# Preparing an attention layer inside the product before it, block by block, with its stores and reloads on GpSimd's queue

## The chip, the cores and the metric

The kernel runs on one core of a Trainium2 chip. The time is device microseconds (us) of one execution on that core. A core has TensorE (PE, matrix products), VectorE (DVE), ScalarE (ACT), GpSimd (POOL) and SyncE (SP), which run their own instruction streams and meet at semaphores, and 16 DMA engines that all queues share. SP and ACT issue DMAs through hardware queues, POOL through a software queue.

## What is computed

Four graph layers over 3125 nodes with 64 features and 100000 edges, each with a layer norm and a ReLU ahead and added to its input:

```
h = relu(layernorm(x));  x = x + smoothing(h)      # three propagations over the edges
h = relu(layernorm(x));  x = x + sage(h)           # one weighted propagation
h = relu(layernorm(x));  x = x + gated_cheb(h)     # two propagations, then (1 - sigmoid(.)) * tanh(.)
h = relu(layernorm(x))
q, k, v = h[src] @ qTrans, h[dst] @ kTrans, h[dst] @ vTrans      # 4 heads of 16
att = exp(clip(sum(q * k, per head), -10, 10))
x = x + segment_sum(att / (segment_sum(att, src)[src] + 1e-8) * v, src)
```

## The kernel before, in words

The nodes are padded to 3200, 25 tiles of 128. The program has three blocks (`nc.Block`), and each ends at a barrier of all five engines: no engine starts the next block before every engine has come to the end of its own stream in this one.

1. `build_matrices` sorts the edges into two dense 3200 x 3200 float matrices in DRAM, `weights_dram` and `counts_dram`. Its scatters are GpSimd's indirect DMAs (L620).
2. `propagating_layers` does six products with these matrices (`prop` 0 to 5; the last, 5, is `CHEB2`). A product goes by seven blocks of columns, `CHUNKS`: six of 512 and one of 128. Four wide blocks (0, 2, 3, 5) are streamed by SP into `ring`, blocks 1 and 4 (`KEPT`) stay in `resident`, block 6 in `last`. On PE a block `n` is 25 matmuls (L969); after the fifth or sixth of them (`s == after`; later in block 6) `by_nodes` (L942) turns the sums of block `n - 1` back to nodes by rows. DVE then finishes the nodes of block `n - 1` (L896 to L905), with ACT's Sigmoid and Tanh between (L773, L775).
3. `attention_layer` has a prologue and a main part. The prologue does for all 25 tiles at once: layer norm (L666 to L674), transposes (L1248), the product with qTrans and kTrans (L1252) and with vTrans (L1257), copies, and the split of q and k into three bf16 parts (L1152, L1155: cast, subtract, cast, subtract, cast). SP stores each part into `parts_dram` (L1073) and loads it again as six groups of 16 rows for q and six for k (L1081), so that one bf16 matmul with 96 rows gives a float-like product. PE waits for all twelve loads (L1262). The main part then goes over chunks of 512 query nodes and, in each, over 25 tiles: scores (L1275), transposed counts (L1282), ACT's exponentials, DVE's clips and products (L1168 to L1176), and values (L1290).

## Time and profile before

| | us |
|---|---|
| median of 3 runs (lowest and highest) | 2656.49 (2653.78 to 2657.03) |
| the profiled execution's own time | 2654.28 |
| its span, first to last instruction | 2652.6 |
| PE busy | 1194.4 (45%) |
| DVE busy | 1843.7 (70%) |
| ACT busy | 776.8 (29%) |
| POOL busy | 1266.3 (48%) |

The shares are means over three stages of a different nature. The first block takes a little over half the span; the change lies at the seam of the second and third. So the stage must be read by itself, in windows of the trace, by its chain of waits: which instruction released which, in order of time. PEq, DVEq and SPq are an engine's sequencer (branches, semaphores, DMA issues).

### The profile page before, as it was taken

What the parts mean: (1) busy time and instruction counts of PE and PEld (TensorE: products, weight loads), DVE (VectorE), ACT (ScalarE), POOL (GpSimd) and SP (SyncE); (2) the same over time, 40 slices, a digit from 0 to 9 for tenths busy, and PEclk for the clock granted to TensorE, in tenths of its full rate; (3) what the DMA queues carried; (4) which work ended last, traced back from release to release, by engine and by line L of the source; (5) the groups of instructions that cost most, each with busy time, mean ns of one, the idle gap of its engine ahead of it and who ended that gap; (6) DMA issues with size and microseconds to landing.
All of it is one profiled execution on the core that took longest, in us unless ns stands there. A gap on an engine that the chain in (4) does not pass through costs nothing. (4 is left out here: it accounts for less than half of the span.)

```text
span 2652.6 us, 40013 instructions
## 1 busy us (share of the span) xinstructions
PE 1194.4 (45%) x12261; PEld 593.1 (22%) x12261; DVE 1843.7 (70%) x3893; ACT 776.8 (29%) x1905; POOL 1266.3 (48%) x973
## 2 busy tenths in 40 slices
PE   1111111111111111111111049999999559989997
PEld 1111111111111111111111013344444313333334
DVE  9988888888888888888888210023211549999997
ACT  0000000132233222311112220000001159999996
POOL 2688888888888888888888600000000000000001
PEclk6555555555555555555555569999999769999997
DMA  7777777588898888767566699889978363333331
GB/s 229 238 202 224 206 210 221 112 212 216 211 226 196 223 211 215 180 139 178 107 165 155 124 372 423 363 362 388 423 286 349 55 120 87 87 87 87 87 87 46
DMA packets 487296, 537.82 MB, mean 203 GB/s; under 512 B 130048, under 2 KB 443709, under 8 KB 469053
## 3 DMA queue, kind: packets, MB, share of 16 engines
q1 hardware_dynamic: 124717, 290.41, 30.2%
q10 hardware_dynamic: 249904, 245.78, 28.7%
q0 software_dynamic: 112608, 0.85, 10.1%
q8 instruction: 28, 0.46, 0.1%
q14 instruction: 39, 0.32, 0.0%
HBM read 368.64 MB, written 168.31 MB: 202 GB/s over the span
## 5 line engine op out<-in xcount | busy, mean ns | idle before, releaser
L620 POOL DMA_INDIRECT table<-amount,cell x782 | 1210.6, 1548 | 294.4 <-issue 278.3
L441 DVE SCALAR_TENSOR_TENSOR equal<-key_row,keys,masks 128x1280 bf16<-128x1280 f32 (+9 forms) x790 | 692.0, 941 | 0.2 <-DVE parts L427 0.2
L573 PE MATMUL totals<-parts_g,equal 128*128 128x6 bf16 x4345 | 128.6, 168 | 1022.8 <-DVE is_tile L450 1022.8
L291 ACT ACTIVATE w_tile<-cells 128x128 f32<-128x128 f32 x600 | 179.2, 301 | 779.5 <-issue 768.8
L573 PEld LDWEIGHTS totals<-parts_g,equal 128*128 128x128 bf16 x4345 | 122.0, 104 | 1034.2 <-DVE is_tile L450 1034.2
L969 PE MATMUL banks<-ring,xs 128*64 128x512 f32 x1200 | 290.9, 601 | 92.7 <-DMA ring<-counts_dram 91.3
L1237 POOL COPY v_tile<-v_all 128x128 f32 x175 | 51.2, 294 | 506.6 <-PE banks_d L1290 433.8
L1227 POOL MEMSET o_t<- 128x64 f32 x1 | 0.2, 151 | 565.2 <-POOLq L731 565.2
L433 DVE SCALAR_TENSOR_TENSOR equal_tail<-key_row,keys,masks 128x1280 bf16<-128x1280 f32 x156 | 235.2, 1545 | 20.6 <-issue 17.5
L1275 PE MATMUL banks_d<-q,k 96*128 (+2 forms) x700 | 194.7, 371 | 75.5 <-DMA k<-parts_dram 46.5
L1122 ACT ACTIVATE att<-banks_d,shift 128x1024 f32<-128x1024 f32 (+1 forms) x175 | 198.7, 1135 | 76.6 <-PE banks_d L1275 76.0
L1127 ACT ACTIVATE att<-att,shift 128x1024 f32<-128x1024 f32 (+1 forms) x175 | 206.6, 1181 | 0.0
L1173 DVE SCALAR_TENSOR_TENSOR att<-att,banks_d 128x1024 f32<-128x1024 f32 (+1 forms) x175 | 190.1, 1086 | 11.4 <-ACT att L1127 4.4
L1176 DVE TENSOR_TENSOR att<-att,banks_d 128x1024 f32<-128x1024 f32 (+1 forms) x175 | 189.0, 1080 | 0.0
L1125 ACT ACTIVATE att<-banks_d 128x1024 f32<-128x1024 f32 (+1 forms) x175 | 183.4, 1048 | 0.0
L1290 PE MATMUL banks_d<-att,v_tile 128*32 128x512 f32 (+1 forms) x1400 | 173.3, 571 | 0.5 <-DVE att L1176 0.5
L458 DVE TENSOR_REDUCE amount<-totals 128x20 f32<-128x60 f32 x79 | 17.3, 219 | 203.9 <-POOLq L634 203.9
L969 PEld LDWEIGHTS banks<-ring,xs 128*64 128x64 f32 x1200 | 93.4, 138 | 263.8 <-issue 149.4
L1168 DVE TENSOR_SCALAR att<-att 128x1024 f32<-128x1024 f32 (+1 forms) x175 | 108.9, 622 | 55.8 <-ACT att L1125 55.1
L969 PE MATMUL banks<-resident,xs 128*64 128x512 f32 x600 | 145.1, 596 | 2.9 <-DMA resident<-counts_dram 2.5
L291 ACT ACT_TABLE_LOAD x1 | 1.3, 1283 | 489.5 <-POOLq L634 489.5
L582 PE MATMUL totals<-carried_parts,equal_tail 128*128 128x6 bf16 x1560 | 54.2, 168 | 199.5 <-DVE carried_parts L478 199.5
(225 smaller groups left out, 1501.0 us busy)
## 6 DMA issues: line engine op xcount, KB each, us to landing
table<-zeros ACTq DMA_DIRECT2D x100, 800.0 KB
cells<-table ACTq DMA_DIRECT2D x24, 3200.0 KB, 12.1
ring<-counts_dram SPq DMA_DIRECT2D x60, 1280.0 KB, 11.7
ring<-weights_dram SPq DMA_DIRECT2D x60, 1280.0 KB, 10.5
key_row<-keys_dram SPq DMA_DIRECT2D x79, 640.0 KB
weights_dram<-w_tile ACTq DMA_DIRECT2D x24, 1600.0 KB
counts_dram<-c_tile ACTq DMA_DIRECT2D x24, 1600.0 KB
count<-counts_dram SPq DMA_DIRECT2D x150, 256.0 KB, 2.9
```

Of the source, the lines that this page charges most:

```text
L291: ins = nc.scalar.activation(w_tile[:, b, s], cells[:, s, :, 0], ACT.Copy, accum_out=deg_parts[:, s, bass.ds(t, 1)])
L433: ins = nc.vector.scalar_tensor_tensor(equal_tail[:, b, i, :], key_row[:, b, :], keys[:, bass.ds(g * G - TAIL + i, 1)], all_mask, ALU.is_e ...
L441: ins = nc.vector.scalar_tensor_tensor(equal[b][:, OWN_AT[j]:OWN_AT[j + 1]], key_row[:, b, j * P:GE], keys[:, bass.ds(g * G + j, 1)], own_ ...
L573: nc.tensor.matmul(sums, equal[b][:, at:at + P], parts_g[:, b, j, :], start=False, stop=True, skip_group_check=True)
L620: nc.gpsimd.indirect_dma_start(out=table, out_offset=bass.IndirectOffsetOnAxis(ap=cell[:, b, j:j + 1], axis=0), in_=amount[:, b, j, :], in ...
L969: ins = nc.tensor.matmul(banks[at:at + D, g % 2, 0:w], xs[:, prop % 2, s], rows, start=s < 2, stop=True, skip_group_check=True)
L1122: nc.scalar.activation(att[:, j, high, 0:W], scores[:, high, 0:W], ACT.Relu, bias=shift[:, 0:1]).then_inc(scores_read[1], 1)
L1125: nc.scalar.activation(att[:, j, low, 0:W], scores[:, low, 0:W], ACT.Exp).then_inc(scores_read[0], 1)
L1127: nc.scalar.activation(att[:, j, high, 0:W], att[:, j, high, 0:W], ACT.Exp, bias=shift[:, 1:2]).then_inc(expd_high, 1)
L1173: nc.vector.scalar_tensor_tensor(att[:, j, high, 0:W], att[:, j, high, 0:W], HI, times, ALU.min, ALU.mult)
L1176: nc.vector.tensor_tensor(att[:, j, low, 0:W], att[:, j, low, 0:W], times, ALU.mult).then_inc(weighted, 1)
L1275: ins = nc.tensor.matmul(scores[:, hd, 0:W], k6[:, hd, bass.ds(t * P, P)], q6[:, hd, bass.ds(ci * BANK, W)], start=True, stop=True)
```

## The change

The attention's prologue moves into the last product of the block before. For a block `n` of nodes:

- DVE, right after it has finished the nodes of block `n`, normalises them (`normalise`, as the earlier layers do), with ACT's Sqrt between, and then splits block `n - 1` (`split`).
- PE, in block `n` (from 2 on), transposes block `n - 2` of `h` after `by_nodes` (`turn_next`), and eight matmuls later projects it (`project`). The last two blocks are done behind the product.
- ACT copies the transposed block (`copy_h`) and the values (`copy_values`, into `k["acc"]`).
- GpSimd, for each block: waits for the three parts, stores them with one DMA, waits until that has landed, and issues twelve loads of 16 rows, each 4 heads x 512 columns (6 x 2 row groups; seven blocks, so 7 stores and 84 loads in place of 3 and 12). It starts when the product's block 1 is done, for the rows lie where `resident` had that block.
- In the attention block, PE waits for `rows_placed[0]` alone, and waits for the later blocks of rows at tiles 4, 8, 12, 16, 20 and 24 of its first chunk, which is written out without a loop (`first=True`). GpSimd copies the values per tile from `acc` into `v_tile`, in strides.
- Some buffers share space for that: `zeros` lies in `k["acc"]`, and `cells`, `w_tile`, the first resident block and the rows all in `k["held"]`.

```diff
+            def copy_h(n):
+                w = CHUNKS[n][1]
+                act.wait_ge(h_turned, n + 1)
+                if n:
+                    act.wait_ge(values_made, n)
+                nc.scalar.copy(h_t[0:D, 0:w], TURN[:, 0:w]).then_inc(h_copied, 1)
...
                         if before[0] == CHEB2:
-                            gates_of(before[1])
+                            if n >= 2:
+                                copy_h(n - 2)
+                            gates_of(n - 1)
+                            root(2, n - 1)
+                            if n >= 2:
+                                copy_values(n - 2)
...
+            def split(n):
+
+                w = CHUNKS[n][1]
+                dve.wait_ge(projected, n + 1)
+                if n >= 2:
+                    dve.wait_ge(rows_stored[n - 2], 16)
+                left = PROJECTED[n % 2][:, 0:w]
+                for i in range(3):
+                    part = parts[:, n % 2, i, 0:w]
+                    if i == 2:
+                        nc.vector.tensor_copy(part, left).then_inc(parts_ready, 1)
+                        break
+                    nc.vector.tensor_copy(part, left).then_inc(parts_step, 1)
+                    dve.wait_ge(parts_step, 4 * n + 2 * i + 1)
+                    nc.vector.tensor_tensor(rest[:, 0:w], left, part, ALU.subtract).then_inc(parts_step, 1)
+                    dve.wait_ge(parts_step, 4 * n + 2 * i + 2)
+                    left = rest[:, 0:w]
+                dve.wait_ge(parts_ready, n + 1)
...
                         link(nc.vector.tensor_tensor(x[:, ts], x[:, ts], narrow, ALU.add))
+                        normalise(ts, tiles, 2 * NC + n)
+                        dve.sem_inc(h_ready, 1)
+                        if n:
+                            split(n - 1)
+            split(NC - 1)
...
+            def project(n):
...
+                nc.tensor.matmul(PROJECTED[n % 2][:, 0:w], k["qk"][:], h_t[0:D, 0:w], start=True, stop=True
+                                 ).then_inc(projected, 1)
+                for j in range(tiles):
+                    ins = nc.tensor.matmul(VALUES[n % 2][:, j * D:(j + 1) * D], h_t[0:D, j * P:(j + 1) * P], k["v"][:],
+                                           start=True, stop=True, skip_group_check=True)
+                ins.then_inc(values_made, 1)
...
+                            if prop == CHEB2 and n >= 2:
+                                turn_next(n - 2)
+                        if prop == CHEB2 and n >= 2 and s == later:
+                            project(n - 2)
             by_nodes(CHEB2, NC - 1)
...
+            for n in (NC - 2, NC - 1):
+                turn_next(n)
+                project(n)
+
+        @block.gpsimd
+        def _(pool):
+            pool.wait_ge(sums_ready, NC * CHEB2 + KEPT[0] + 1)
+            for n, (c0, w) in enumerate(CHUNKS):
+                cols = slice(c0, c0 + w)
+                pool.wait_ge(parts_ready, n + 1)
+                pool.dma_start(parts_dram[:, :, :, :, cols].rearrange("i w h d n -> (w h d) i n"), parts[:, n % 2, :, 0:w]
+                               ).then_inc(rows_stored[n], 16)
+                pool.wait_ge(rows_stored[n], 16)
+                for side, part_of in ((1, KPART), (0, QPART)):
+                    for i in range(NPART):
+                        pool.dma_start(placed[side][i * HD:(i + 1) * HD, :, cols],
+                                       parts_dram[part_of[i], side, :, :, cols].rearrange("h d n -> d h n")
+                                       ).then_inc(rows_placed[n], 16)
...
-            layer_norm(nc, dve, link, x, h, tmp, stat, var_ready, std_ready, 0)
-            dve.sem_inc(h_ready, 1)
...
-            pe.wait_ge(v_copied, 1)
             pe.wait_ge(consts_set, 2)
-            pe.wait_ge(rows_placed, 16 * 2 * NPART)
+            pe.wait_ge(rows_placed[0], 16 * 2 * NPART)
...
+                    if first:
+                        for t in range(2, T):
+                            if t * P % BANK == 0:
+                                pe.wait_ge(rows_placed[t * P // BANK], 16 * 2 * NPART)
+                            step(t, t % RING, t // RING)
+                        return
```

PE in the last product, its fifth block (`resident`), before:

```order
L969 MATMUL banks<-resident,xs 64x512 [waits sums_read]
L969 MATMUL banks<-resident,xs 64x512 x4
L942 MATMUL banks<-cheb,y_t 128x128 [waits sums_read,post_read]
L942 MATMUL banks<-cheb,y_t 128x128 x3
L969 MATMUL banks<-resident,xs 64x512 x20
```

and now, the same place (L1063 is the product, L1009 `by_nodes`, L1022 `turn_next`, L1032 and L1035 `project`):

```order
L1063 MATMUL banks<-resident,xs 64x512 [waits sums_read]
L1063 MATMUL banks<-resident,xs 64x512 x4
L1009 MATMUL banks<-cheb,y_t 128x128 [waits sums_read,post_read]
L1009 MATMUL banks<-cheb,y_t 128x128 x3
L1022 MATMUL banks<-ident,h 64x128 [waits h_ready_c,h_copied_c]
L1022 MATMUL banks<-ident,h 64x128 x3
L1063 MATMUL banks<-resident,xs 64x512 x8
L1032 MATMUL banks<-h_t,qk 128x512 [waits values_copied,parts_step,h_copied_c]
L1035 MATMUL banks<-v,h_t 128x64 x4
L1063 MATMUL banks<-resident,xs 64x512 x12
```

Nine more instructions stand in the block: four transposes, one wide product and four narrow ones.

ACT in the last product, one block of it, before (L773 and L775 are Sigmoid and Tanh):

```order
L773 ACTIVATE term<-acc 128x4x64 [waits gate_ready]
L775 ACTIVATE term<-h 128x4x64
```

and now, a block from 2 on:

```order
L802 COPY h_t<-banks 64x512 [waits values_made,h_turned_c]
L793 ACT_TABLE_LOAD
L793 ACTIVATE term<-acc 128x4x64 [waits gate_ready]
L795 ACTIVATE term<-h 128x4x64
L788 ACT_TABLE_LOAD
L788 ACTIVATE stat<-stat 128x4 [waits var_ready]
L807 COPY acc<-banks 128x256 [waits values_made]
```

The function tables are loaded twice in each block, once ahead of Sigmoid and once ahead of Sqrt.

GpSimd between the barrier after `build_matrices` and the attention's first copies, before:

```order
L1224 UNCONDITIONAL_BRANCH [waits barrier_Pool_Activation_PE_DVE_SP_gather]
L1227 MEMSET o_t 128x64
L1228 MEMSET v_all 128x3200
L1230 MEMSET v_all 128x100 [waits v_cleared]
```

and now (the first two of seven blocks, and the seventh with what follows it):

```order
L1093 DMA parts_dram<-xs 128x3x512 [waits parts_ready,sums_ready]
L1098 DMA held<-parts_dram 16x4x512 [waits rows_stored0]
L1098 DMA held<-parts_dram 16x4x512 x11
L1093 DMA parts_dram<-xs 128x3x512 [waits parts_ready]
L1098 DMA held<-parts_dram 16x4x512 [waits rows_stored1]
L1098 DMA held<-parts_dram 16x4x512 x11
```

```order
L1093 DMA parts_dram<-xs 128x3x128 [waits parts_ready]
L1098 DMA held<-parts_dram 16x4x128 [waits rows_stored6]
L1098 DMA held<-parts_dram 16x4x128 x11
L751 UNCONDITIONAL_BRANCH
L1280 UNCONDITIONAL_BRANCH [waits barrier_Pool_Activation_PE_DVE_SP_gather]
L1284 MEMSET v_tile 128x640
```

All 91 DMAs stand ahead of the barrier in GpSimd's stream, each store behind the twelve loads of the block before it.

## Rows read from the trace of the kernel before

**Rows 1.** Chain that ended last, 1950 to 2165 us: start us, us, what.
```profile
2074.74 1.83 DVE stat L666
...
2084.93 4.34 PE banks_d L1248 x25
...
2108.08 22.40 DMA parts_dram<-qk_part
...
2130.84 19.23 DMA k<-parts_dram
...
2150.22 0.06 PEldq L1263
...
2150.44 2.97 DMA count<-counts_dram
```

**Rows 2.** Waits, 2060 to 2156 us: waited for, us in total, times, longest.
```profile
PE banks_d L1275 <- DMA k<-parts_dram: 46.5, 1, 46.5
...
DVE stat L666 <- PEq L731: 0.5, 1, 0.5
```

**Rows 3.** Timeline of PE, 1960 to 2075 us: start us, us, instruction.
```profile
1966.62 0.60 PE L916 MATMUL banks<-ident,h 128*64 128x128 f32 x4
...
2020.37 1.16 PE L942 MATMUL banks<-cheb,y_t 128*128 128x128 f32 x8
...
2056.98 1.16 PE L942 MATMUL banks<-cheb,y_t 128*128 128x128 f32 x8
...
2069.20 1.53 PE L969 MATMUL banks<-last_chunk,xs 128*64 128x128 f32 x24
```

**Rows 4.** Timeline of all engines, 2040 to 2165 us.
```profile
2044.58 1.16 PE L942 MATMUL banks<-cheb,y_t 128*128 128x128 f32 x8
...
2045.85 0.69 DVE L896 TENSOR_TENSOR term<-banks,scale 128x512 f32<-128x512 f32 x1 [8.66 <-PE banks L942]
...
2048.58 0.42 DVE L905 TENSOR_TENSOR x_nodes<-x_nodes,term 128x256 f32<-128x256 f32 x1
...
2074.71 1.28 ACT L1109 ACT_TABLE_LOAD   x1 [1.02 <-PEq L731]
...
2086.03 0.58 ACT L1046 COPY h_t_d<-banks_d 64x512 f32<-64x512 f32 x1 [3.42 <-PE banks_d L1248]
```

**Rows 5.** Groups by line, 2071 to 2156 us: busy us, mean ns, idle before.
```profile
L1257 PE MATMUL banks_d<-v,h_t_d 64*128 64x64 f32 x50 | 8.5, 350 | 0.7 <-DVE qk_t L1049 0.7
...
L1155 DVE TENSOR_TENSOR qk_t<-qk_t,qk_part 128x3200 f32<-128x3200 f32 x2 | 7.0, 3493 | 0.1
...
L1252 PE MATMUL banks_d<-h_t_d,qk 64*128 64x512 f32 (+1 forms) x14 | 5.6, 551 | 0.0
L1152 DVE CAST qk_part<-qk_t 128x3200 bf16<-128x3200 f32 x3 | 5.5, 1827 | 0.2
...
L1049 DVE COPY qk_t<-banks_d 128x512 f32<-128x512 f32 x3 | 2.1, 691 | 3.4 <-PE banks_d L1252 3.4
```

**Rows 6.** Line 840 alone: ns min/median/max, first and last start us.
```profile
L840 DVE TENSOR_REDUCE stat<-x_nodes x14: 219/420/421, 1753.6 to 1909.7; 128x4 f32<-128x256 f32 x12, 128x1 f32<-128x64 f32 x2
```

**Rows 7.** Line 620, GpSimd's DMAs, alone.
```profile
L620 POOL DMA_INDIRECT table<-amount,cell x782: 1546/1546/2582, 47.7 to 1508.0; - x196
```

**Rows 8.** Timeline of POOL, 1000 to 1040 us.
```profile
1007.12 1.55 POOL L620 DMA_INDIRECT table<-amount,cell  x1 [0.30 <-issue]
1008.97 1.55 POOL L620 DMA_INDIRECT table<-amount,cell  x1 [0.30 <-issue]
```

**Rows 9.** Line 1081 alone, SP's loads of the rows.
```profile
L1081 SPq DMA_DIRECT2D k<-parts_dram x6: 303/427/467, 2105.1 to 2130.8; - x6
```

**Rows 10.** Line 1073 alone, SP's stores of the parts.
```profile
DMA to landing us min/median/max: 3.3/4.7/22.4
```

**Rows 11.** DMA, 2108 to 2130.8 us.
```profile
DMA packets 631, 3.30 MB, mean 145 GB/s; under 512 B 115, under 2 KB 115, under 8 KB 630
```

More of the change, by code:

```diff
@@ L72, in by_chunk, with rows_of @@
     return dram[c0 * NR:(c0 + w) * NR].rearrange("(p s c) -> p s c", p=P, s=T)
+def rows_of(k):
+    half = T * BANK // 2
+    return [k["held"][0:NPART * HD, w * half:(w + 1) * half].bitcast(BF16).rearrange("p (h n) -> p h n", h=HEADS)
+            for w in range(2)]
 def gnn_layers(nc, x, src, dst, edge_weight, W_self, b_self, W_neigh, b_neigh,
@@ L90, in gnn_layers @@
             "stat": sb("stat", [P, 3, T], F32),
+            "acc": sb("acc", [P, T, D], F32),
+            "held": sb("held", [P, T * BANK], F32),
             "ident": sb("ident", [P, P], F32),
@@ L101, in gnn_layers @@
         }
+        parts_dram = nc.dram_tensor("parts_dram", [3, 2, HEADS, HD, NR], BF16, kind="Internal").ap()
+        rows_placed = [ctx.enter_context(nc.semaphore(f"rows_placed{n}")) for n in range(len(CHUNKS))]
         with ExitStack() as c:
@@ L154, in build_matrices @@
     amount = sb("amount", [P, 2, G, 2], F32, c)
-    cells = sb("cells", [P, T, P, 2], F32, c)
-    w_tile, c_tile = sb("w_tile", [P, 2, T, P], F32, c), sb("c_tile", [P, 2, T, P], F32, c)
+    cells = k["held"][:, 0:2 * NR].rearrange("p (s c two) -> p s c two", c=P, two=2)
+    w_tile = k["held"][:, 2 * NR:4 * NR].rearrange("p (b s c) -> p b s c", b=2, c=P)
+    c_tile = sb("c_tile", [P, 2, T, P], F32, c)
     deg_parts = sb("deg_parts", [P, T, T], F32, c)
@@ L684, in propagating_layers @@
     xs = sb("xs", [P, 2, T, D], F32, c)
-    acc = sb("acc", [P, T, D], F32, c)
+    acc = k["acc"]
     gates = (acc, h)
@@ L692, in propagating_layers @@
     ring = sb("ring", [P, PIECES, PIECE, BANK], F32, c)
-    resident = sb("resident", [P, len(KEPT), T, BANK], F32, c)
+    resident = [k["held"][:].rearrange("p (s c) -> p s c", c=BANK), sb("resident", [P, T, BANK], F32, c)[:]]
+    rest = term[:].rearrange("p t f -> p (t f)")
+    parts = xs[:, 0].rearrange("p t f -> p (t f)")[:, 0:3 * BANK].bitcast(BF16).rearrange("p (b n c) -> p b n c", b=2, n=3)
+    placed = rows_of(k)
     last = sb("last_chunk", [P, T, P], F32, c)
@@ L714, in propagating_layers @@
     last_landed = sem("last_landed")
+    h_ready, h_turned, h_copied = sem("h_ready_c"), sem("h_turned_c"), sem("h_copied_c")
+    projected, values_made, values_copied = sem("projected"), sem("values_made"), sem("values_copied")
+    parts_step, parts_ready = sem("parts_step"), sem("parts_ready")
+    rows_stored = [sem(f"rows_stored{n}") for n in range(len(CHUNKS))]
     def tiles_of(n):
@@ L944, in by_nodes, with turn_next @@
                 ins.then_inc(post_filled, 1)
+            def turn_next(n):
+                ts = tiles_of(n)
+                if n:
+                    pe.wait_ge(h_copied, n)
+                else:
+                    pe.wait_ge(turned_copied, 2 * NC)
+                pe.wait_ge(h_ready, n + 1)
+                for j, t in enumerate(range(ts.start, ts.stop)):
+                    ins = nc.tensor.transpose(TURN[:, j * P:(j + 1) * P], h[:, t], k["ident"][:])
+                ins.then_inc(h_turned, 1)
+            def project(n):
+                w, tiles = CHUNKS[n][1], CHUNKS[n][1] // P
+                pe.wait_ge(h_copied, n + 1)
+                if n >= 2:
+                    pe.wait_ge(parts_step, 4 * (n - 2) + 2)
+                    pe.wait_ge(values_copied, n - 1)
+                nc.tensor.matmul(PROJECTED[n % 2][:, 0:w], k["qk"][:], h_t[0:D, 0:w], start=True, stop=True
[4 more added lines that the diff above has]
+                ins.then_inc(values_made, 1)
             for prop in range(6):
@@ L951, in _ @@
                     after = (T // 2 if n == NC - 1 else PIECE) // 2 * 2 + 1 - g % 2
+                    later = after + 8
                     for s in range(T):
@@ L960, in _ @@
                                 pe.wait_ge(kept_landed[KEPT.index(n)][q], 16 * (prop // 3) + 16)
-                            rows = resident[:, KEPT.index(n), s]
+                            rows = resident[KEPT.index(n)][:, s]
                         else:
@@ L1107, in _ @@
         def _(act):
-            act.wait_ge(var_ready, 1)
-            nc.scalar.activation(stat[:, 2], stat[:, 1], ACT.Sqrt).then_inc(std_ready, 1)
-            copy_banks(act, nc.scalar.copy, 0)
             act.wait_ge(consts_set, 2)
@@ L1315, in steps, with chunk @@
                 return scores_of, tiles, values_of
-            def chunk(ci, width, next_width):
-                scores_of, tiles, values_of = steps(ci, width)
+            def chunk(ci, width, next_width, first=False):
+                scores_of, tiles, values_of = steps(ci, width, first)
                 tiles()
@@ L1329, in _ @@
                 steps(0, 4)[0](t)
-            with pe.Fori(0, SC - 1) as ci:
+            chunk(0, 4, 4, first=True)
+            with pe.Fori(1, SC - 1) as ci:
                 chunk(ci, 4, 4)
```

119 lines of the change are left out of this document (34 added, 85 removed).

## The prediction, on record before the changed kernel ran

> **What bounds the kernel now.** I read the page's slices first. DVE and GpSimd fill the first stage, PE the second and DVE the third, and between the second and the third lie slices with every engine low: the attention's prologue. What it costs is read from the chain of waits [rows 1]. The barrier holds DVE for 0.5 us [rows 2], from 2074.2 on; then one engine at a time works: layer norm (from 2074.7), transposes and projections (from 2084.9), the split (to 2108.1) [rows 1]. From there to 2150.1 nothing computes: the third store lands 22.40 us after its issue and the last load of rows 19.23 us after its own. PE passes its gate at 2150.2 [rows 1], after 46.5 us of waiting [rows 2]. So 76 us lie between the two stages, 42 of them DMA. The gate is the one point that counts: behind it the attention is DVE's, tile by tile, and its instructions are not touched, so that a gate passed x us earlier is worth x us. In the last product PE is the bound; its blocks follow at (2056.98 - 2020.37) / 3 = 12.2 us [rows 3].
>
> **What the change adds to the product (paid).** Per wide block PE gets four transposes, 0.60 [rows 3]; the wide product, 5.6 / 6.25 = 0.9; four narrow pairs, 8.5 / 25 x 4 = 1.4 [rows 5]. The sum is 2.9 us. Blocks 2 to 6 of the product each carry one set, so it ends 5 x 2.9 = 14.5 us later, at 2070.7 + 14.5 = 2085.2 [rows 3], with blocks 15.1 us apart. All of it is PE's; that the product is not slowed further I take from DVE having 8.66 us idle in a block [rows 4], and the bound of this is nothing to 14.5 us if a DMA wait of PE hides some.
>
> **When the parts of a block are ready.** `by_nodes` of a block starts at 2044.58 and DVE adds the result to x until 2049.0 [rows 4], 4.4 us later. ACT now loads a table between (1.28 [rows 4]); it comes after ACT's copy of h (0.58 [rows 4]) and so holds Sigmoid up by about 1.1. The normalisation is five operations of 0.42 [rows 6], with small ones and links between, 2.9 us; the Sqrt table loads beside it. The split by block: cast and subtract from PSUM at 0.69 each (the nearest is L1049, 691 ns), then from SBUF 1827 x 512 / 3200 = 0.29, 3493 x 512 / 3200 = 0.56 and 0.29 [rows 5], 2.6 with the links. Block 0 is projected in PE's third block, at about 2026, earlier than DVE gets there. So its parts are ready at 2020.4 + 4.4 + 1.1 + 2.9 + 2.6 = 2031.4, the next ones 15 us apart (2046, 2061, 2076), block 4's at about 2090, and blocks 5 and 6, behind the product with two further table loads and a chain through four engines, at about 2096 and 2097.
>
> **GpSimd's queue.** It decides. Per block it issues a store, waits until that has landed, and issues twelve loads; 91 DMAs all stand ahead of the barrier, which no engine passes without GpSimd. So the waits for single blocks in the attention's first chunk never bind: when PE gets there, all loads have been issued. The trace has no plain DMA from this queue. The nearest rows:
> - one load (64 rows of 1 KB). Below: SP's issue of 64 rows, 0.43 [rows 9]. Above: GpSimd's indirect DMA of 128 rows, 1.55 [rows 7] with 0.30 between, a period of 1.85 [rows 8]. That one reads its addresses as well. I take half of it for half the rows, 0.93.
> - the store (384 rows): issue 1.85, as one indirect DMA (0.34 as SP's, 5.6 for three times the rows). Landing: 3.3, the least of L1073 [rows 10], which moved twice the bytes.
>
> A block costs S = 1.9 + 3.3 + 12 x 0.93 = 16.3 us, more than the 15 at which blocks come. The queue is never empty after the first: it ends at 2031.4 + 7 x 16.3 = 2145.5. With the barrier (0.5) and DVE's constants, now behind it (0.4), PE's gate is passed at 2146.4 instead of 2150.2: -3.8 us. The first count tile and the exponentials' table load follow the gate as before. GpSimd's one small copy per tile stays one small copy. The first chunk without a loop and the shared buffers I cost at nothing: the one stands beside DVE's work, the others move no instruction; if PE fetched its longer code late, it would be a few us.
>
> So the change removes 76 us of serial work, pays 14.5 to the product and about 12 behind it, and the queue gives most of the rest back. Profiled: span 2652.6 - 3.8 = 2648.8, own time 2650.5. The runs' median stands 2.2 above the profiled time: 2656.5 - 3.8 = 2652.7, so **2653 us**. About 0.2% (5.3 us) is what a measurement here can tell from no change.
>
> Every us in S is 7 us in the end. It breaks even at S = (2150.2 - 0.9 - 2031.4) / 7 = 16.8, a load of 0.97 us. The bounds: with SP's issue times S = 0.34 + 3.3 + 5.2 = 8.8, and the queue waits for the parts until block 4 (2090 + 3 x 8.8 = 2116.4, the gate at 2117.3): -33 us, 2624. With the dearest of all, S = 5.6 + 3.3 + 22.2 = 31.1: 2031.4 + 217.7 = 2249: +100 us.
>
> **A rule that speaks against it.** L1152, a cast from SBUF, took 1827 ns for 3200 elements, L1155 3493 [rows 5]: the cast runs at nearly twice the rate. By the Trainium skill ("SBUF — State Buffer", "SBUF: two separate sides"), GpSimd cannot write descriptors while VectorE runs an operation in its two-port mode. No row here shows plain DMAs of GpSimd beside such a cast. If that held in full, two casts of 0.29 would add 0.6 to each S, 4 us in all, and turn the -3.8 into 0. The same skill ("DMA: Bandwidth & Descriptors", "Latency and other measured facts") gives about 1 us to the first byte of a DMA from this queue; taken as a load's issue time, as an estimate, it would give S = 17.2 and +3 us.
>
> **Rivals.**
> - Cheap issue. The 1.55 us are mostly for the addresses of an indirect DMA; a plain one of 64 rows costs 0.65 (between 0.43 and 0.93), the store 0.5. S = 11.6, and blocks wait for their parts: block 4 ends at 2101.6, block 6 at 2124.8, the gate at 2125.7, -24.5 us, **2632**. For it: SP needs only 0.43 for the same rows [rows 9]. Against it: the software queue's only row is four times that [rows 7].
> - Dear issue, the other side. The cost is nearly one per DMA, not per row: 1.25, midway between 0.65 and the 1.85 of rows 8. S = 1.9 + 3.3 + 15 = 20.2, the queue ends at 2172.8, the gate at 2173.7, +23.5 us, **2680**. GpSimd would then work for 140 us while the other engines stand at the barrier for 75. It decides from 0.97 us on. For it: 782 indirect DMAs never took less than 1546 ns [rows 7]. Against it: these have twice the rows and more to read.
> - Store behind loads, slower too. In the old prologue the DMA engines were full at 145 GB/s [rows 11], 9 GB/s each, and the third store took 22.4 us behind the loads of 6400 B rows [rows 1]. By bytes, a block's loads (786 KB) take 5.4 us at that rate, less than their issue, and the next store waits for the last one alone. If a row of 1 KB cost half of the 6400 / 9.06 = 706 ns of a long one, 48 rows per engine would take 17 us, the next store would land behind them, and S = 17 + 1.9 + 3.3 = 22: +39 us, **2695**. It decides from 0.24 us per row. Against it: a DMA's cost by bytes fits the other transfers.
>
> **Chances.** My forecast (S from 15.3 to 17.7) 0.34, cheap issue 0.28, dear issue 0.30, store behind loads 0.08. Of the forecast's 0.34, 0.13 is faster by over 0.2% (S under 16.05), 0.20 within it, 0.01 slower. So faster 0.41, same 0.20, slower 0.39. The range goes from the lower bound's side, 2624, to the third rival, 2695; that leaves out the dearest issues and little else. The forecast's own range is 2646 to 2659.
>
> **What would show it.** PE's blocks 2 to 5 of the last product 15 us apart and its end near 2085 (right), or 12 to 13 apart (a DMA wait hid it). First store of parts from GpSimd near 2031. The period of GpSimd's loads: 0.93 as forecast, under 0.8 the first rival, over 1.1 the second. From a store's issue to the first load 3 to 5 us; 10 or more is the third. All engines but GpSimd idle from about 2098 to the barrier. No wait of PE for rows in the first chunk. A gate of PE at 2146 with the attention of the same length; the forecast is wrong if the attention itself changes by more than 3 us, or if the first two blocks of the program, untouched in their instructions, move.

## The result and the profile after

The changed kernel takes 2637.40 us (median of 4 runs, 2635.66 to 2641.44), the kernel before 2655.39 beside it (median of 4, 2653.78 to 2657.03). The ratio is 0.993, with a 95% interval of 0.9917 to 0.9943: 18 us or 0.7% faster. The prediction said 2653 and faster with a chance of 0.41; the result lies in its range (2624 to 2695), but outside the forecast's own (2646 to 2659). The profiled execution took 2636.98 us, its span is 2635.3.

The first score of attention is the gate. PE's timeline around it, after (start us, us, instruction):

```profile
2102.49 0.52 PE L1035 MATMUL banks<-v,h_t 64*128 64x64 f32 x2
2135.27 1.01 PE L1317 MATMUL banks_d<-held 96*128 96x512 bf16 x2 [32.25 <-ACTq L1184]
```

Before, the first score stood at 2150.47, right behind the gate of [rows 1]. So 15.2 of the 17.3 us of span come from an earlier gate, and 2.1 from attention itself (500.0 instead of 502.1 us; on these 2.1 see the experiment with the looped chunk). Who is waited for now? The waits from 2030 to 2140 us, after (waited for: us in total, times, longest), to be read beside [rows 2]:

```profile
POOL held L1098 <- DMA parts_dram<-xs: 37.5, 7, 17.2
...
PE banks_d L1317 <- ACTq L1184: 32.3, 1, 32.3
...
DVE zero_row_d L1213 <- PEq L751: 28.9, 1, 28.9
...
POOL v_tile L1284 <- POOLq L751: 7.7, 1, 7.7
```

PE, ACT and DVE all stand at the barrier for about 30 us, and no engine waits for the rows of a block in attention. The engine that holds the barrier is GpSimd. Its whole timeline from the first parts on:

```profile
2040.56 0.86 POOL L1093 DMA_DIRECT2D parts_dram<-xs  x1 [521.69 <-DVE xs L905]
2050.08 6.36 POOL L1098 DMA_DIRECT2D held<-parts_dram  x12 [8.67 <-DMA parts_dram<-xs]
2056.43 0.78 POOL L1093 DMA_DIRECT2D parts_dram<-xs  x1
2074.40 6.09 POOL L1098 DMA_DIRECT2D held<-parts_dram  x12 [17.20 <-DMA parts_dram<-xs]
2080.48 0.77 POOL L1093 DMA_DIRECT2D parts_dram<-xs  x1
2083.73 6.09 POOL L1098 DMA_DIRECT2D held<-parts_dram  x12 [2.48 <-DMA parts_dram<-xs]
2089.82 0.77 POOL L1093 DMA_DIRECT2D parts_dram<-xs  x1
...
2118.21 0.77 POOL L1093 DMA_DIRECT2D parts_dram<-xs  x1
2120.72 6.09 POOL L1098 DMA_DIRECT2D held<-parts_dram  x12 [1.74 <-DMA parts_dram<-xs]
2134.56 0.63 POOL L1284 MEMSET v_tile<- 128x640 f32 x1 [7.75 <-POOLq L751]
```

The loads alone (duration min/median/max in ns, first and last start):

```profile
L1098 POOL DMA_DIRECT2D held<-parts_dram x84: 514/514/692, 2050.1 to 2126.3; - x84
```

The reader is to see four things. After its first store GpSimd never waits for parts; how near it comes to waiting is told in the part on the prediction. A block's cycle in the quiet part is 2089.82 - 2080.48 = 9.3 us, not 16.3: a load's issue is 6.09 / 12 = 0.51 us and a store's 0.77. The first two stores are waited for during 8.67 and 17.20 us instead of 2.48. And there are 7.75 us between the end of the last load's issue and the barrier. What the core's DMA engines did meanwhile stands in the windows of after (start:end, length, then busy time of PE, PEld, DVE, ACT and POOL, TensorE's granted clock, DMA share, GB/s):

```profile
2041.00:2050.00 9.00, 9.00 (x47) 3.87 (x43) 3.54 (x8) 4.45 (x6) 0.41 (x1) 1.00 1.00 391
2056.00:2074.00 18.00, 18.00 (x96) 7.93 (x94) 8.03 (x18) 5.41 (x9) 1.21 (x2) 1.00 0.97 286
2100.00:2127.00 27.00, 1.51 (x5) 1.06 (x5) 4.88 (x14) 0.94 (x4) 20.11 (x39) 0.50 0.38 100
2128.50:2134.50 6.00, 0.00 (x0) 0.00 (x0) 0.00 (x0) 0.00 (x0) 0.00 (x0) 0.50 0.00 0
```

The two slow stores went while the DMA engines were full (share 1.00 and 0.97), mostly with SyncE's stream of matrix tiles; beside the second one block 0's own loads were under way too, which needed up to 15.0 us to land. And in the last 6 us ahead of the barrier nothing is done by any engine or any DMA.

Line 632 alone is the scatter of the first stage, GpSimd's indirect DMA (duration min/median/max in ns, first and last start), the counterpart of [rows 7]:

```profile
L632 POOL DMA_INDIRECT table<-amount,cell x782: 1550/1559/2572, 48.3 to 1517.3; - x196
```

This stage's instructions are the same, and yet its median is 13 ns longer, and its last scatter starts at 1517.3 instead of 1508.0. PE's first product behind it starts 9.2 us later (1569.03 against 1559.84), and in the last product `by_nodes` of block 1 still comes 8.3 later (2028.63 against the 2020.37 of [rows 3]). PE's last product itself went by rows such as these:

```profile
2029.62 0.60 PE L1022 MATMUL banks<-ident,h 128*64 128x128 f32 x4
...
2033.73 1.12 PE L1032 MATMUL banks<-h_t,qk 64*128 64x512 f32 x2
2034.70 1.00 PE L1035 MATMUL banks<-v,h_t 64*128 64x64 f32 x8
...
2073.39 0.60 PE L1022 MATMUL banks<-ident,h 128*64 128x128 f32 x4
```

Three blocks take 2073.39 - 2029.62 = 43.8 us, 14.6 each, against 12.2 in [rows 3].

### The profile page after: what moved, and what is told of

Read it like the earlier page. It is cut to its first block and busy times, and to the rows that moved or that the text cites. A ratio compares the mean times of both kernels' runs of the same rounds, so it can differ in the third digit from the quotient of the medians.

```text
span 2635.3 us, 40047 instructions
## 1 busy us (share of the span) xinstructions
PE 1193.1 (45%) x12261; PEld 590.7 (22%) x12261; DVE 1857.5 (70%) x3958; ACT 795.0 (30%) x1929; POOL 1312.5 (50%) x1064
## 5 line engine op out<-in xcount | busy, mean ns | idle before, releaser
L303 ACT ACTIVATE held<-held 128x128 f32<-128x128 f32 x600 | 179.2, 301 | 787.2 <-issue 776.4
L1063 PE MATMUL banks<-ring,xs 128*64 128x512 f32 x1200 | 290.5, 600 | 93.0 <-DMA ring<-counts_dram 91.7
L1093 POOL DMA_DIRECT2D parts_dram<-xs x7 | 5.5, 783 | 521.7 <-DVE xs L905 521.7
L1294 POOL COPY v_tile<-acc 128x64 f32 x175 | 41.5, 238 | 441.1 <-PE banks_d L1332 440.5
L1317 PE MATMUL banks_d<-held 96*128 (+2 forms) x700 | 192.9, 366 | 65.7 <-ACT att L1195 32.4
L1063 PEld LDWEIGHTS banks<-ring,xs 128*64 128x64 f32 x1200 | 92.9, 137 | 261.9 <-issue 147.7
L836 ACT COPY y_t<-banks 128x512 f32<-128x512 f32 (+1 forms) x42 | 22.7, 540 | 340.6 <-PE banks L1063 340.6
L925 DVE TENSOR_TENSOR xs<-banks,scale 128x256 f32<-128x256 f32 (+1 forms) x14 | 5.5, 396 | 164.1 <-PE banks L1009 164.1
```

The costliest lines, as they stand in the source:

```text
L303: ins = nc.scalar.activation(w_tile[:, b, s], cells[:, s, :, 0], ACT.Copy, accum_out=deg_parts[:, s, bass.ds(t, 1)])
L1063: ins = nc.tensor.matmul(banks[at:at + D, g % 2, 0:w], xs[:, prop % 2, s], rows, start=s < 2, stop=True, skip_group_check=True)
L1317: ins = nc.tensor.matmul(scores[:, hd, 0:W], k6[:, hd, bass.ds(t * P, P)], q6[:, hd, bass.ds(ci * BANK, W)], start=True, stop=True)
```

## The experiments

Eleven kernels ran. The question was where the queue's 28 saved us went, and whether GpSimd is the engine to issue these DMAs. Beside each time stands its ratio to the kernel before of the same chip, with the 95% interval.

**SyncE issues instead of GpSimd.** The changed kernel; the loop of stores and loads stands at the end of SyncE's part of the same block, behind its last tile of the matrix:

```
-        @block.gpsimd
-        def _(pool):
-            pool.wait_ge(sums_ready, NC * CHEB2 + KEPT[0] + 1)
+            sp.wait_ge(sums_ready, NC * CHEB2 + KEPT[0] + 1)
...
-                pool.dma_start(parts_dram[...]
+                sp.dma_start(parts_dram[...]
```

> The changed kernel with its 7 stores and 84 loads issued by SP, behind SP's last stream, instead of by GpSimd; all else as changed. In the changed kernel GpSimd issued a load each 0.51 us and a block of rows took 9.35 us (0.77 store, 2.48 landing, 6.1 loads); its last load was issued at 2126.8 and the barrier opened 7.7 us later. Theory A (GpSimd's own end of stream costs some 7 us, and the queue the rest): SP issues a load in 0.43 us, the last parts are ready at about 2105.7 in the changed trace's time, the last block follows one block behind it (3.3 + 5.2), and the barrier opens 0.5 us after the last issue: PE's gate about 13 us earlier than in the changed kernel. If the first stage also returns to its old length, 9 us more: 2615 to 2625 us. Rival B (the barrier waits for the rows' landing or for something that any queue has): the gate moves by 0 to 5 us, 2632 to 2637 us. Rival C (hardware queue fills the DMA engines with 16-partition loads at 145 GB/s, stores land late behind them): not faster or slower than the changed kernel.

Measured: 2617.02 us (4 runs), 0.9864 [0.9849, 0.9879]: 20.4 us below the changed kernel's median, or 18.6 when each is taken against the kernel before on its own chip. Its scatters, SyncE's timeline and GpSimd's next instruction:

```profile
L632 POOL DMA_INDIRECT table<-amount,cell x782: 1546/1547/2512, 47.6 to 1508.3; - x196
```

```profile
2048.22 0.53 SPq L783 DMA_DIRECT2D parts_dram<-xs  x1
2058.26 5.67 SPq L788 DMA_DIRECT2D held<-parts_dram  x12
...
2106.34 0.43 SPq L783 DMA_DIRECT2D parts_dram<-xs  x1
2108.26 5.46 SPq L788 DMA_DIRECT2D held<-parts_dram  x12
2114.82 32.66 SPq L1165 DMA_DIRECT2D count<-counts_dram  x16
```

```profile
2114.12 0.63 POOL L1281 MEMSET v_tile<- 128x640 f32 x1 [604.30 <-POOLq L751]
```

The first score stands at 2114.84, 20.4 us earlier than in the changed kernel (attention then takes 501.0 instead of 500.0). These 20.4 us come apart in three. The first stage is 9.0 shorter (last scatter 1508.3 against 1517.3). SyncE's last issue ends at 2113.72, which is 2126.81 - 9.0 - 2113.72 = 4.1 earlier than GpSimd's would without that shift, though SyncE, busy with the matrix until 2048.1, issues its first store 16.7 us later by that measure: a load costs it 0.46 (5.46 / 12), a block in the quiet part 8.1 to 9.1. And GpSimd's first clear of attention, at 2114.12, follows this end by 0.4 instead of 7.75. Together 9.0 + 4.1 + 7.35 = 20.4. So the projection inside the product is worth 36.6 us, and about half of that hangs on who issues its DMAs. Theory A had the size, and rivals B and C fall.

**The shared buffers alone.** The kernel before, with only the buffers of the change (`held` and `acc` in place of `zeros`, `cells`, `w_tile`, the old `acc`, the first resident block, `q6` and `k6`); nothing is moved in time:

```
-    q6, k6 = sb("q6", [NPART * HD, HEADS, NR], BF16, c), sb("k6", ...)
+    q6, k6 = rows_of(k)
...
-    cells = sb("cells", [P, T, P, 2], F32, c)
+    cells = k["held"][:, 0:2 * NR].rearrange(...)
```

> The kernel before with only the shared buffers of the change (zeros in acc; cells, w_tile, the first resident block and the rows in held). Question: the first stage became 9 us longer in the changed kernel (GpSimd's indirect DMAs 1559 ns instead of 1546, 782 of them). Theory A, the place of the buffers does it: indirect DMAs at about 1559 ns, total +8 to +10 us over before. Rival B, it comes with GpSimd's plain DMAs or differs from run to run: indirect DMAs at 1546 ns, total as before within 3 us.

Measured: 2653.89 us (11 runs), 1.0002 [0.9993, 1.0011], scatters at 1546 ns with the last at 1509.2. The addresses cost nothing; the 9 us are not theirs. (The profiled execution was the slowest of the eleven, 2662.06 us, and its scatters are as short as those of the kernel before; it is met again under the looped chunk.)

**The old prologue's DMAs from GpSimd.** The kernel before, with its 15 stores and loads of the rows (the only ones of [rows 9, 10]) issued by GpSimd:

```
-            def keep(part_no):                         # in SyncE's attention
-                sp.dma_start(parts_dram[part_no]...
+            def keep(part_no):                         # in GpSimd's attention
+                pool.dma_start(parts_dram[part_no]...
```

> The kernel before with its old prologue, where GpSimd instead of SP issues the 3 stores and 12 loads of whole rows (6400 B). Theory A (the cost of GpSimd's plain DMA is about 0.5 to 0.8 us each and rows land at the same pace as from SP): the prologue is bound by landing, so within 3 us of before if the first stage stays. If plain DMAs in GpSimd's stream are what lengthens the first stage's indirect DMAs (1559 instead of 1546 ns): +9 us on top. Rival B (each plain DMA costs 1.3 to 1.9 us): the twelve loads cost 15 to 23 us of issue, of which the DMA landing hides most, total +3 to +8 us without any change in the first stage.

Measured: 2662.20 us (5 runs), 1.0035 [1.0022, 1.0049]: 8.6 us slower. Line 620 of it:

```profile
L620 POOL DMA_INDIRECT table<-amount,cell x782: 1549/1558/2557, 48.3 to 1518.1; - x196
```

Its plain DMAs run 600 us after the last scatter, in another block of the program, and still each scatter is 12 ns longer and the last starts 10 us later. This separates the effect from anything else in the change. A second place in this trace bears on the rule on the two-port mode. The timeline of all engines:

```profile
2113.88 1.55 POOL L1222 DMA_DIRECT2D q<-parts_dram  x3
2115.42 3.09 POOL L1222 DMA_DIRECT2D k<-parts_dram  x3
2116.58 1.83 DVE L1132 CAST qk_part<-qk_t 128x3200 bf16<-128x3200 f32 x1
```

Three loads take 1.55 us where no cast runs, and 3.09 beside one: GpSimd was held up by about 1.5 us, nearly the cast's 1.83. By the Trainium skill ("SBUF — State Buffer", "SBUF: two separate sides") GpSimd can't write descriptors while VectorE works in its two-port mode; this row agrees. In the changed kernel the casts of a full block take 0.43 to 0.69 us and no load of 84 took more than 692 ns; its seven groups of loads took 43.3 us together, seven of the shortest would be 42.6. So the rule cost it about 0.7 us in all at most, not the 4 us that the prediction allowed for.

**GpSimd last at the barrier, without a DMA.** The kernel before, in which GpSimd waits for DVE's last addition and then clears one column:

```
+        @block.gpsimd
+        def _(pool):
+            pool.wait_ge(finished, 1)
+            nc.gpsimd.memset(pool_mark[:], 0.0)
```

> The kernel before, in which GpSimd waits for DVE's last operation of the second block, clears one column and only then ends its stream there; no DMA of GpSimd's in that block. It tells what the 7.7 us between GpSimd's last load and the barrier in the changed kernel are. Theory A, they belong to the DMAs (a drain of the software queue): the barrier opens 0.5 to 1 us after GpSimd's clear, total +0.5 to +1.5 us over before. Rival B, they belong to GpSimd's change of block (branch, instruction fetch) and are hidden when it ends early: the barrier opens 5 to 8 us after the clear, total +5 to +8 us.

Measured: 2653.44 us (10 runs), 1.0001 [0.9992, 1.0011]. GpSimd's timeline:

```profile
2073.43 0.10 POOL L912 MEMSET pool_mark<- 128x1 f32 x1 [563.58 <-DVEq L907]
2073.82 0.15 POOL L1234 MEMSET o_t<- 128x64 f32 x1 [0.29 <-POOLq L732]
```

The barrier is open 0.3 us behind the clear. That GpSimd comes last costs nothing; the 7.75 us come with the DMAs that it has issued.

**Two marks behind the last load.** The changed kernel:

```
+            nc.gpsimd.memset(pool_mark[:, 0:1], 0.0)
+            pool.wait_ge(rows_placed[len(CHUNKS) - 1], 16 * 2 * NPART)
+            nc.gpsimd.memset(pool_mark[:, 1:2], 0.0)
```

> The changed kernel with two marks on GpSimd at the end of its block: a small clear right behind its last load, then a wait until the loads of block 6 have landed, then a second small clear. Time should be that of the changed kernel (2637, within 2). Theory A (the end costs a fixed stretch): the first mark stands within 0.2 us of the end of the last load's issue, the second some 2 us later, and the barrier opens only 5 to 8 us behind the second mark: the engine's end of a block with DMAs in it costs that. Theory B (GpSimd's own issue work is still going on while the records show the instruction over): the first mark itself stands late, 5 us or more behind the last load, and the barrier opens 0.3 us behind the second mark. Theory C (waiting for its DMAs to be done): the gap shrinks by what the wait for the landing takes, and the barrier opens at the same time as before with the second mark 2 us before it or less.

Measured: 2638.03 us (one run). GpSimd's timeline:

```profile
2121.59 6.06 POOL L1099 DMA_DIRECT2D held<-parts_dram  x12 [1.75 <-DMA parts_dram<-xs]
2127.64 0.12 POOL L1102 MEMSET pool_mark<- 128x1 f32 x1
2129.12 0.10 POOL L1104 MEMSET pool_mark<- 128x1 f32 x1 [1.36 <-DMA held<-parts_dram]
2136.96 0.63 POOL L1288 MEMSET v_tile<- 128x640 f32 x1 [7.75 <-POOLq L752]
```

Theory A: the first mark comes at once, the second 1.5 us later when the loads have landed, and then the same 7.75 us pass. The engine is free, its transfers are over, and the barrier still waits; the stretch begins behind the last instruction, whatever that is.

**One plain DMA.** Three kernels ask how many it takes. First the kernel with SyncE's queue, whose very last load is GpSimd's:

```
+                        if (n, side, i) == (len(CHUNKS) - 1, 0, NPART - 1):
+                            continue
...
+            pool.wait_ge(rows_stored[n], 16)
+            pool.dma_start(placed[0][(NPART - 1) * HD:NPART * HD, ...]
```

> The e1 kernel, but the very last load (block 6, q side, third part) is issued by GpSimd, its only plain DMA. If one plain DMA anywhere in GpSimd's stream is enough for the longer scatters: the indirect DMAs take 1560 ns in the mean instead of 1549, the last of them starts at about 1518 instead of 1508, and the median is 2617 + 9 and, if the end of its block costs its 7 us as soon as there is one DMA in it, + 7 more: about 2633. If the scatters lengthen with the number of such DMAs: 1549 ns and no shift. If the end costs nothing with one DMA: gate at 2114 plus the shift.

Measured: 2621.37 us (4 runs), 0.988 [0.9864, 0.9895]; 4.4 us above the kernel without it. The scatters' median is 1553 ns, the last starts at 1513.4. Of the end of the block it says little: SyncE's own last load ends at 2117.18, behind GpSimd's (2113.09), and the barrier opens 0.4 behind that. My expectation had overlooked that cover. It does say that the end is not 7.75 us with one DMA, for that would have opened the barrier at 2120.8. The other two stand on the kernel with late loads, told next, where nothing covers it: GpSimd issues the store of block 6, ahead of the barrier, or that of block 0 (`BY_POOL = 0`), far from it.

```
+BY_POOL = 6
...
+                if n != BY_POOL:
                     sp.dma_start(parts_dram[...]
...
+            n, (c0, w) = BY_POOL, CHUNKS[BY_POOL]
+            pool.wait_ge(parts_ready, n + 1)
+            pool.dma_start(parts_dram[..., c0:c0 + w]...
```

> The kernel with late loads (2602.1 us), with one plain DMA on GpSimd: the store of block 6, the last DMA before the barrier (about 2098.5 plus the shift). Theory (a fixed stretch at the end of a block in which GpSimd issued DMAs): barrier not with SyncE's last issue but 4.5 to 8 us behind GpSimd's store, and the scatters of the first stage longer as with one plain DMA before (1553 ns, last one +5 us): median 2602 + 5 + 5 to 8, about 2613. Rival (the 7.75 us in the changed kernel come from the number of DMAs, 91, such as a queue that is emptied): with one DMA the barrier opens 0.4 to 1 us behind the store: median 2602 + 5 = 2607.

> The kernel with late loads (2602.1 us), with one plain DMA on GpSimd: the store of block 0, 55 us before the barrier, so that no stretch at the end of its block can show. Theory (one plain DMA in GpSimd's stream lengthens the indirect DMAs of an earlier stage): they take 1553 ns in the mean against 1546, the last one starts at 1513 to 1514 instead of 1508.8, and the median is about 2607. Rival (the shift seen before with one such DMA was chance between runs, or hangs on where in the program it stands): 1546 ns, 2602.

Measured: 2610.24 us with block 6's store (4 runs, 0.9826 [0.9804, 0.9847]), 2608.50 with block 0's (4 runs, 0.9818 [0.9796, 0.9839]), against 2602.11 without (4 runs and more each, but on another chip; against the kernel before of each chip they are 7.7 and 6.0 us dearer). The scatters, of block 6's and of block 0's kernel:

```profile
L635 POOL DMA_INDIRECT table<-amount,cell x782: 1547/1556/2493, 47.6 to 1514.3; - x196
```

```profile
L635 POOL DMA_INDIRECT table<-amount,cell x782: 1547/1556/2579, 48.0 to 1515.8; - x196
```

One store of 384 KB, issued 520 us after the last scatter, lengthens 782 scatters by 10 ns each and costs 6.4 us at the end, which the scatters' shift (1515.8 against 1508.8) covers. With block 6's store (96 KB) it is 8.1 by the medians; in the profiled executions the first score comes 6.3 later than without (2107.35 against 2101.03), of which the shift is 5.5. Over all kernels (scatter's median, last start): without plain DMAs 1546 or 1547 ns and 1508.0 to 1509.2 in seven kernels; with one 1553 to 1556 ns and 1513.4 to 1515.8 in three; with 15 or 91 of them 1558 and 1559 ns, 1518.1 and 1517.3. Most of it is there with the first one. And the end of the block, in block 6's kernel:

```profile
2102.98 0.84 POOL L1109 DMA_DIRECT2D parts_dram<-xs  x1 [587.10 <-DVEq L753]
2106.64 0.63 POOL L1312 MEMSET v_tile<- 128x640 f32 x1 [2.82 <-POOLq L753]
```

The same store alone:

```profile
DMA to landing us min/median/max: 3.3/3.3/3.3
```

The barrier opens 2.8 us behind the end of GpSimd's issue, while SyncE's last issue ended at 2103.64. But the store landed only at 2102.98 + 3.3 = 2106.3, and the barrier opens 0.4 behind that. So the end is not fixed at 7.75, as the theory had it; with one DMA it fits a wait until that DMA has landed, which the rival's queue that is emptied would be. With 91 DMAs such a wait is not enough, for behind the second mark all had landed and 7.75 us still passed. Whether their number makes that, or that most are loads, no run here parts.

**Late loads: the version that beats both.** In the kernel with SyncE's queue the barrier waits for loads of rows that attention's first chunk wants only at its 20th and 24th tile. Here the loads of blocks 5 and 6 stand behind it, two ahead of each count load from the sixth on:

```
+            def place_late(t):
+                for n, side, i in late[each * (t - RING):each * (t - RING + 1)] if t >= RING else ():
+                    sp.wait_ge(rows_stored[n], 16)
+                    sp.dma_start(placed[side][i * HD:(i + 1) * HD, :, cols],
...
             def chunk(ci, width, first=False):
                 for t in range(T):
+                    if first:
+                        place_late(t)
```

> The e1 kernel (SyncE issues stores and reloads), with the 24 loads of blocks 5 and 6 moved behind the barrier into attention's own SyncE stream: two of them ahead of each count load from the sixth to the seventeenth of the first chunk. Theory: in e1 what set the gate was SyncE's issue of 24 to 30 loads behind the last parts; without them the last thing before the barrier is store 6, issued when the parts of block 6 are there (about 2097.5 in the time of before), so the barrier opens at about 2099 and the first score stands at about 2100 instead of 2114.7: span about -14 against e1, median about 2603 us. Rival (late loads in the way): 0.43 us of issue each, two ahead of a count load, hold count tiles back or rows of block 5 come later than tile 20 of the first chunk: attention's part grows from 500.3 by several us and the median stays at 2608 or more. Rival (the product's end is the bound anyway): the last transposes and the vector parts wait for something else behind 2097.5, gate not before 2105.

Measured: 2602.11 us (5 runs), 0.9805 [0.9792, 0.9818]: 51.7 us below the kernel before and 35.3 below the changed one's median (33.7 when each is taken against the kernel before on its own chip). SyncE's and PE's timelines:

```profile
2093.46 5.46 SPq L792 DMA_DIRECT2D held<-parts_dram  x12
2098.96 0.96 SPq L784 DMA_DIRECT2D parts_dram<-xs  x2
2100.86 2.57 SPq L1184 DMA_DIRECT2D count<-counts_dram  x5
2103.47 1.22 SPq L1174 DMA_DIRECT2D held<-parts_dram  x2
```

```profile
2095.37 0.53 PE L1051 MATMUL banks<-v,h_t 64*128 64x64 f32 x2
2101.03 1.86 PE L1336 MATMUL banks_d<-held 96*128 96x512 bf16 x4 [5.13 <-ACTq L1203]
```

The first score stands at 2101.03, 13.8 us earlier than with all loads ahead (2114.84), and 5.1 us after PE's last projection. In the first 80 us of attention PE waits for no load of rows.

**Block 4's loads late too.** The same kernel with

```
-LATE = 5
+LATE = 4
```

> The kernel with late loads (2602.1 us), with block 4's 12 loads behind the barrier too, three ahead of each of twelve count loads. In the trace with two blocks late, SyncE's last stores stood at 2098.96 because the loads of block 4 ran until 2098.92; without these the stores of blocks 5 and 6 go when their parts are there (about 2096.5 and 2098). Theory: the barrier opens up to 1 us earlier, median 2601 to 2602. Rival: three loads ahead of a count load (1.4 us) hold the count tiles up: 2603 or more.

Measured: 2603.77 us (5 runs, 2599.4 to 2609.09), 0.9798 [0.9776, 0.982]: no difference that these runs can tell. Its profiled run has the first score at 2098.89, 2.1 earlier as meant, and loses it in attention: the granted clock there falls to 0.86 or 0.93 in every third stretch of 25 us, where the other kernel's is 1.00 until 2545. Windows of the one and of the other (the columns as above):

```profile
2170.00:2195.00 25.00, 22.49 (x118) 7.67 (x119) 22.16 (x24) 21.76 (x23) 1.74 (x7) 0.86 0.28 79
2195.00:2220.00 25.00, 23.00 (x140) 8.01 (x139) 24.86 (x27) 25.00 (x27) 1.89 (x8) 1.00 0.30 86
```

```profile
2170.00:2195.00 25.00, 21.61 (x130) 7.28 (x129) 24.00 (x26) 23.58 (x25) 1.76 (x8) 1.00 0.29 84
```

Two of its five runs took 2609, two 2601 or less. The late loads don't set this: the profiled execution of the kernel with only the shared buffers, which has none, shows the same dips (0.86 or 0.93 in every third such stretch from 2230 to 2555) and the same length of attention, 508.2 us. What does is open.

**The looped first chunk.** The kernel with SyncE's queue; PE waits for all rows ahead of attention and runs its first chunk in the loop, as before the change:

```
-            pe.wait_ge(rows_placed[0], 16 * 2 * NPART)
+            for landed in rows_placed:
+                pe.wait_ge(landed, 16 * 2 * NPART)
...
-            chunk(0, 4, 4, first=True)
-            with pe.Fori(1, SC - 1) as ci:
+            with pe.Fori(0, SC - 1) as ci:
```

> The e1 kernel with the first chunk of attention looped again on TensorE, as before the change, all rows waited for ahead of it. In the trace of the changed kernel attention took 500.3 us from its first score to the end against 502.4 before. If the unrolled first chunk is what made it shorter, this kernel's attention takes 502.4 and its median is 2619. If the two are the same, 2617 and 500.3: the 2.1 us come from elsewhere, such as count tiles or rows of scores that are ready earlier.

Measured: 2618.34 us (4 runs), 0.9867 [0.9852, 0.9883], the same as 2617.02. From its first score (2116.49) to the end are 498.8 us, less than the 501.0 of the kernel beside it. So the unrolled chunk isn't what made attention 2.1 us shorter. With the same instructions in it, this stretch took 502.1, 500.4, 500.8 and 508.2 us in four kernels of the old form, and 498.6 to 501.0 in eight of the new and 508.2 in one: 2.1 us is no more than what one execution differs from another. The length goes with the granted clock: in stretches of 25 us it stayed at 1.00 between the first and the last 50 us of attention in the changed kernel (500.0) and fell to 0.93 three times in the kernel before (502.1). That the clock is the cause is not shown.

## Why the prediction was right, and where its steps were not

The direction and the range held, and so did the first half of the mechanism: the gate is where GpSimd's queue ends plus a barrier. The second half, that each us of a block's cycle counts seven times because the queue is never empty, did not. How much of the hit is luck must be said: the range spans 71 us, "faster" had a chance of 0.41 against 0.39 for "slower", and the forecast of -3.8 us met -18. The result lies near the rival "cheap issue" (2632), partly by luck as well: its gate was 2125.7 against a measured 2135.27, for its cycles of 11.6 us were too dear and two costs that it lacked, 8.3 and 7.6 us, are more than that. Predicted: 2031.4 + 7 x 16.3 + 0.9 = 2146.4. Measured: 2040.56 + 86.25 + 7.75 + 0.71 = 2135.27. Step by step:

- **PE's product.** 2.9 us more per block were forecast, 14.6 - 12.2 = 2.4 measured. Transposes 0.60 as forecast, the wide pair 1.12 less overlap, but the eight narrow matmuls 1.00 instead of 1.4: inside the product's stream they cost 0.12 each, not the 0.17 of [rows 5]. It was not hidden.
- **Parts ready.** The first store came at 2040.56; forecast 2031.4. Of these 9.2 us, 8.3 stood already at `by_nodes` of block 1 and come from the first stage. The chain of additions behind it took 11.9 instead of 11.0: DVE's split 3.1 instead of 2.6 (a cast of 512 elements from SBUF took 0.43, not the 0.29 that a division of the wide one gave), and 0.6 from its end to the store.
- **A load's issue, the step that failed.** 0.93 us, as half of an indirect DMA with its pause [rows 8], against 0.514 measured (84 loads, 514 to 692 ns). The rows had bounds of 0.43 (SyncE's, [rows 9]) and 1.55, and the truth lay just above the lower one. What an indirect DMA costs did not carry over to a plain one here, for all that both are GpSimd's. The store's issue was 0.77 instead of 1.85. The cheap rival had 0.65 and 0.5.
- **A store's landing.** 3.3 forecast. In the quiet part issue and wait are 0.77 + 2.48 = 3.25 together; the first two took 9.5 and 18.0 beside a stream that filled the DMA engines. The first had no loads of rows ahead of it, so the matrix tiles alone do that much; with the second, tiles and block 0's loads were both under way. In the quiet part the rival "store behind loads" fails: twelve loads just issued leave the wait at 2.48.
- **The queue that never empties.** Cycle by cycle the queue took 15.9, 24.0, 9.3, 9.7, 9.4, 9.3 and 8.6: 86.25 in all, against 114.1 forecast. But a cycle of 9.3 is less than the 14.6 at which blocks come, so a queue of such cycles waits for parts up to block 4, as the lower bound and the cheap rival had it. DVE had block 4's parts ready at 2097.4, and their store started at 2099.50, only 2.1 later, where the very first store started 0.6 behind its parts. By this estimate the two slow stores cost 1.5 us at the end, and what counts is block 4's parts and three cycles behind them: 2097.4 + 2.1 + 27.3 + 8.5 = 2135.3. This is also why SyncE, which starts 16.7 us later, ends earlier: from block 4's store to the last issue it takes 2113.72 - 2089.34 = 24.4 us against 27.3.
- **The barrier.** 0.5 forecast, as in [rows 2], where GpSimd had issued no plain DMA. 7.75 measured, and by the two marks neither issue nor transfer.
- **The first stage.** That one of the first two blocks of the program moves was named as what would make the forecast wrong, and the first moved by 9.3 us. By that sign the forecast itself failed.

In the forecast's own terms, GpSimd's queue was 27.9 too dear (the loads' issue 34.8 and the stores' 7.8 too dear, the landings 14.4 too cheap; the rest is that 16.36 was rounded to 16.3). With +9.2 for the first store and +7.6 for the barrier this comes to -11.1 at the gate; the attention's 2.1 us and the runs' medians make the rest. Without the two missing costs, 8.3 of the first stage and 7.6 of the barrier, the change would have brought about 34 us, nearly the lower bound's -33, and with SyncE's queue it brings 36.6.

Two of the prediction's figures don't come out of its own terms. The third rival's S is 22.2, which gives +37.5 us, not +39. And S up to 17.7 would reach 2662, not the 2659 at which the forecast's own range ends (that is S = 17.2).

The step that all 91 DMAs stand ahead of the barrier, so that the waits for single blocks never bind, was right, and it was the hint to the better kernel: such waits are only worth their code when the loads may come late.

## What to carry to other kernels

Price each kind of DMA by its own row, and a kind that has none by an experiment; half the period of an indirect DMA on the same engine was 1.8 times the truth. Before a cycle is multiplied by the number of blocks, compare it with the time at which blocks come: if it is shorter, only the cycles behind the last late arrival count. Before work is moved to an engine because it is idle, ask what the move does to that engine's other blocks and to its exit from a block: here two costs outside the moved work ate 16 of 34 us. And loads that have a wait of their own need not stand ahead of a barrier; what is wanted last can be issued behind it, between the loads of the next stage.

## What the runs showed of the hardware that was not expected

- Plain DMAs of GpSimd in a later block of the program lengthen its indirect DMAs of an earlier one: 7 to 10 ns with one, 12 to 13 with 15 or 91, on 1546, or 5 to 10 us over 782 of them. Why is open.
- A block in which GpSimd issued 91 plain DMAs ends 7.75 us behind its last instruction, with every engine and DMA engine idle in the last 6 us, and also when the last load has landed before. With one such store ahead of the barrier it ended 2.8 us behind the issue, which is 0.4 behind the landing. What it waits for isn't settled.
- SyncE issues these loads in 0.43 us, GpSimd in 0.51 (64 rows of 1 KB); the stores in 0.43 and 0.77.
- A VectorE cast of 1.83 us held up GpSimd's issue of one load by about 1.5 us.
- A 384 KB store that is waited for until 3.25 us after its start in the quiet took 9.5 and 18 us beside a stream that filled the DMA engines, the second with loads of its own queue ahead of it.
